# Six small DMA issues per batch moved from SyncE's queue to ScalarE's queue

## The reference

```python
x = x + xattn0(ctx, ctx, layernorm(x), ssm_kernel, D, 8)   # long convolution of k*v products, times q
x = x + ffn0(layernorm(x), gate_w, gate_b, val_w, val_b, out_w, out_b)  # activations and weights quantised, silu gate
x = x + xattn1(layernorm(x), ctx, mask, mask, Wq, bq, Wk, bk, Wv, bv)   # 16 heads of 8, softmax over 256 keys
x = x + ffn1(layernorm(x), Wc, temperature, genes, Wd, Wu, norm_w, scale)  # top 32 of 512 logits, softmax, gene mix
```

## Time and profile before

| | us |
|---|---|
| three runs | 569.9, 570.42, 573.87 (median 570.42) |
| the profiled execution | 567.63 |
| its span in the trace | 565.8 |
| busy in the span: PE, DVE, ACT, POOL | 458.6 (81%), 453.2 (80%), 350.7 (62%), 373.4 (66%) |

### The profile page before, as it was taken

The page is one execution under the profiler, slowest core; times in us unless marked ns, Lnnn a source line. Parts: engine busy times, 40 slices in busy tenths (PEclk is TensorE's granted clock), DMA queues, the critical chain, the costliest instruction groups (busy, mean ns, idle before and its releaser), DMA issues.

```text
span 565.8 us, 10986 instructions
## 1 busy us (share of the span) xinstructions
PE 458.6 (81%) x3587; PEld 257.0 (45%) x3587; DVE 453.2 (80%) x885; ACT 350.7 (62%) x607; POOL 373.4 (66%) x692
## 2 busy tenths in 40 slices
PE   1787699998987988989889898898988887778442
PEld 1576567776754543444344444444434333322110
DVE  4595579998679879799799998999989998973451
ACT  1469534333131588787788878888877877776431
POOL 6466399999887657677778777786655752341332
PEclk9987989999889899999899999999999999996875
DMA  6971011001451256565464646537636753411100
GB/s 195 370 190 25 22 56 30 17 12 48 100 115 32 64 98 137 114 113 129 91 112 110 112 124 135 103 102 158 134 96 133 150 118 102 67 28 30 51 9 19
DMA packets 93932, 54.48 MB, mean 96 GB/s; under 512 B 16610, under 2 KB 93602, under 8 KB 93876
## 3 DMA queue, kind: packets, MB, share of 16 engines
q1 hardware_dynamic: 93876, 53.78, 41.2%
HBM read 35.84 MB, written 17.42 MB: 94 GB/s over the span
## 4 chain that ended last, share of the span: by engine, by line
PE 38%; DVE 18%; issue 13%; POOL 10%; ACT 10%; DMA 6%; SPq 4%; POOLq 2%; DVEq 0%; ACTq 0%
PE pair L280 11%; DVE w_int L1669 6%; PE bank L501 5%; ACT cT L1323 5%; PE pair L488 3%; PE bank L393 3%; PE bank L530 2%; PE pair L472 2%; DMA w_raw<-w_int 2%; DVE st L1607 2%; DVE toep L1721 2%; POOL kv L949 2%; PE bank L420 2%; DMA yT<-in_x 2%; PE bank L554 1%
## 5 line engine op out<-in xcount | busy, mean ns | idle before, releaser
L1669 DVE TENSOR_REDUCE w_int<-pair 128x4 f32<-128x1024 f32 x128 | 155.2, 1213 | 23.7 <-PE pair L472 23.0
L1323 ACT ACTIVATE cT<-pair 128x1024 f32<-128x1024 f32 x128 | 131.1, 1024 | 36.1 <-PE pair L488 33.7
L280 PE MATMUL pair<-kv,toep 128*128 128x256 f32 x384 | 103.2, 414 | 8.6 <-POOL kv L949 6.3
L280 PEld LDWEIGHTS pair<-kv,toep 128*128 128x128 f32 x384 | 76.3, 208 | 25.7 <-issue 7.3
L949 POOL TENSOR_TENSOR kv<-cT 128x512 f32<-128x512 f32 x64 | 66.1, 1038 | 20.2 <-PE pair L280 14.4
L488 PE MATMUL pair<-w_raw,KS 57*128 57x256 bf16 x512 | 50.9, 277 | 33.4 <-ACT cT L1323 24.0
L501 PE MATMUL bank<-cT,v_aug 128*32 128x256 f32 x1024 | 71.1, 396 | 0.2 <-ACT qT L1331 0.2
L1494 DVE TENSOR_TENSOR prod<-pair,qT 128x512 f32<-128x512 f32 x64 | 43.9, 685 | 22.6 <-PE pair L280 21.8
L472 PE MATMUL pair<-KS,w_raw 54*128 54x256 bf16 x512 | 50.4, 275 | 10.8 <-DVE w_int L1669 10.4
L488 PEld LDWEIGHTS pair<-w_raw,KS 57*128 57x128 bf16 x512 | 16.9, 94 | 72.3 <-ACT cT L1323 54.3
L1039 POOL TENSOR_TENSOR w_raw<-w_raw 128x512 f32<-128x512 f32 x32 | 40.7, 1271 | 8.5 <-ACT w_raw L1278 7.3
(11 more groups left out here) (174 smaller groups left out, 938.7 us busy)
## 6 DMA issues: line engine op xcount, KB each, us to landing
w_raw<-scr_q SPq DMA_DIRECT2D x32, 192.0 KB
KS<-scr_k SPq DMA_DIRECT2D x32, 192.0 KB
scr_q<-w_int SPq DMA_DIRECT2D x16, 192.0 KB, 2.4
scr_k<-w_int SPq DMA_DIRECT2D x16, 192.0 KB, 2.6
scr_o<-qT SPq DMA_DIRECT2D x64, 36.0 KB
yT<-in_x SPq DMA_DIRECT2D x4, 512.0 KB, 7.6
ctx_all<-in_ctx SPq DMA_DIRECT2D x4, 512.0 KB, 8.1
x_b<-in_x SPq DMA_DIRECT2D x16, 128.0 KB, 4.5
```

Source lines behind the costliest of these rows:

```text
L280: mm = pe.matmul(bank[:, lh * n:(lh + 1) * n], toep[:, h, (lh - sh) * P:(lh - sh + 1) * P], rhs[:, sh, :], start=(sh == 0), stop=(sh == lh))
L1323: act.activation(probs[g % 4].rearrange("p j l -> p (j l)"), SC[:], ACT.Exp).then_inc(s("scores_free"), 1)
L1669: dve.tensor_reduce(neg_max[:, :, 2 * g:2 * g + 2].rearrange("p t j -> p j t"), M[:].rearrange("p (j t s) -> p j t s", t=KL, s=L), AX.X, A ...
```

## The change

`write_attention` and `load_max_rows` are moved word for word from the program of SP to that of ACT. On ACT, the four writes stand behind `copy_hidden_T(.., 1)` and ahead of `value_operand`, the two loads behind `tanh_gate(.., 0)` and ahead of `exp_left`, in both loops. The semaphores, the addresses and the sizes stay the same.

```diff
@@ sync
-                sp.wait_ge(s("o_free"), turn_o["maxima", b])
-                for j in range(2):
-                    sp.dma_start(QS[b % 3][HALF * j + ROW_MAX:HALF * j + ROW_MAX + 3, :, :],
-                                 nm_rows[3 * GRP * j:3 * GRP * (j + 1), :]).then_inc(s(f"max_rows{b % 2}_loaded"), 16)
...
-                    sp.dma_start(scr_o[k].rearrange("(q j) d l -> j d q l", j=4)[jj],
-                                 o_quad[32 * jj:32 * jj + HD + 1, :, :]).then_inc(s(f"o{k}_written"), 16)
...
-                write_attention(m - 10)
                 load_bias_terms(m - 1)
-                load_max_rows(m - 9)
@@ scalar
+            def write_attention(b):
+                if not live(b):
+                    return
+                k = b % 2
+                act.wait_ge(s("o_free"), turn_o["values", b, 3])
+                if b >= 2:
+                    act.wait_ge(s(f"o_nat{k}_loaded"), 32 * (b // 2))
+                for jj in range(4):
+                    act.dma_start(scr_o[k].rearrange("(q j) d l -> j d q l", j=4)[jj],
+                                 o_quad[32 * jj:32 * jj + HD + 1, :, :]).then_inc(s(f"o{k}_written"), 16)
+
+            def load_max_rows(b):
+                if not live(b):
+                    return
+                act.wait_ge(s("o_free"), turn_o["maxima", b])
+                for j in range(2):
+                    act.dma_start(QS[b % 3][HALF * j + ROW_MAX:HALF * j + ROW_MAX + 3, :, :],
+                                 nm_rows[3 * GRP * j:3 * GRP * (j + 1), :]).then_inc(s(f"max_rows{b % 2}_loaded"), 16)
...
                 copy_hidden_T(m - 4, 1)
+                write_attention(m - 10)
                 value_operand(m - 8)
                 copy_max_rows(m - 9)
                 tanh_gate(m - 3, 0)
+                load_max_rows(m - 9)
                 exp_left(m - 12)
```

More of the change, by code:

```diff
@@ L788, in load_stacked_qk @@
                     sp.dma_start(KS[n][rows, :, :], scr_k[k].rearrange(stacked, g=GRP, j=2)[j]).then_inc(loaded, 16)
-            def load_max_rows(b):
-                if not live(b):
-                    return
-                sp.wait_ge(s("o_free"), turn_o["maxima", b])
-                for j in range(2):
-                    sp.dma_start(QS[b % 3][HALF * j + ROW_MAX:HALF * j + ROW_MAX + 3, :, :],
-                                 nm_rows[3 * GRP * j:3 * GRP * (j + 1), :]).then_inc(s(f"max_rows{b % 2}_loaded"), 16)
[L798 to L805, removed]
-                    sp.dma_start(scr_o[k].rearrange("(q j) d l -> j d q l", j=4)[jj],
-                                 o_quad[32 * jj:32 * jj + HD + 1, :, :]).then_inc(s(f"o{k}_written"), 16)
             def load_attention(b):
```

## The result

The changed kernel took 598.8 us in the median of four runs (593.49 to 599.75), the kernel before 571.43 us in four runs beside it (569.9 to 573.87). The ratio is 1.046, 95% interval [1.042, 1.050]: 27.4 us slower. The few executions of a slower state are left out of all medians here.

A forecast was written before the change was run, and what follows sets the result against it. The prediction took a round through PE, DVE and ACT to bound the kernel, SP having time to spare. 8.4 + 3.4 + 1.0 + 4.5 = 17.3 us slower gave 587.7 us on the median, range 575 to 603.

The forecast's parts named there:

- Price of an issue: Each issue on ACT was taken to cost what SP's rows show: 0.32 us a write, 0.77 us a load.
- Held or beside: Whether ACT's issue waits for the activation ahead to end (held, 22.5 us in all) or does not (beside, 12.0 us).
- Steady rows, 1.4 us each: Rows m = 12 to 17 of the first loop: DVE's `top_first` late by 0.9 to 1.9 us a row, 8.4 us together.
- the middle that was taken: In rows m = 12 to 17, 1.4 us a row, between 0.9 for issues overlapping activations and 1.9 without overlap.
- Rows m = 10, 11 and 18: Here ACT's waits for PE cover part of the issues; together with row m = 9, 3.4 us was forecast.
- Row m = 19: The writes go in ahead of `value_operand` and delay `copy_max_rows`, which has no slack: 1.0 us taken, between 0.5 and 1.4.
- Late rows, 0.9 us each: Rows m = 20 to 24: uncovered writes on ACT delay `copy_max_rows`, the loads and PE's `scores`, 4.5 us together.
- Row m = 9, 0 to 0.5 us: Only the loads are issued by ACT in this row: 0.5 us if held, 0 if issued beside the activation.
- the 2.99 us freed become waiting: On SP, the issue time saved per row goes into its wait ahead of the load of denominators; gain nothing.
- dearer: Rival, 597 to 611 us: SP's and ACT's issues hold each other up, 1.2 us in 14 rows, or cost more; chance 0.13.
- Nothing from the clock: No time was put down for TensorE's granted clock, 1.00 in both windows; its fall would make the prediction wrong.
- almost free: Rival, 570.4 down to 564 us: issues cost ACT almost nothing and late rows' loads start earlier; chance 0.10.

The follow-up runs named there:

- e9: Changed kernel with one wait added on SP, in row m = 9 only, until batch 0's row maxima have landed; 592.43 us.
- e1: Kernel before with only the four writes (`write_attention`) moved to ACT, the loads staying on SP; 584.7 us, ratio 1.017.
- e2: Kernel before with only the two loads (`load_max_rows`) moved to ACT, the writes staying on SP; 582.8 us, ratio 1.021.
- e4: Kernel before, all its transfers left on SP, plus six spare issues of the same shapes per batch on ACT, to scratch memory; 588.08 us, ratio 1.030.
- e8: Changed kernel with eight extra matmuls of 256 columns ahead of `logits_product`, into a free bank that nobody reads; 596.63 us.
- e6: Kernel before, everything on SP, with the two loads put ahead of the four writes in both loops; 601.1 us, ratio 1.052.
- e10: Kernel before with only the first load of rows m = 20 to 24 issued by ACT, directly behind its copy; 565.62 us, ratio 0.991.
- e3: Changed kernel with SP again waiting for the copy of the row maxima, where the loads had stood, in both loops; 596.07 us.

## Why the prediction was right, and where its size was off

The forecast was 17.3 us slower, the result is 27.4. The mechanism holds: nothing is gained on SP's queue, and ACT, held by its issues, passes the delay on. The size was short by 10.1 us, for terms that the sum lacked or had near nothing.

- **Price of an issue: right.** 342 and 729 ns in the median against SP's 320 and 774. By the page "Perfetto Trace Analysis" of the Trainium skill, section "DMA Instruction — HWDGE (DVE, Sync)", the profiled time of an issue ends when the sequencer is free for its next instruction. The trace agrees for ACT's queue: the four writes end at 338.35 and `value_operand` starts at 338.46.
- **Held or beside: open in the prediction, now settled as beside.**
- **Steady rows, 1.4 us each: right in size, but not by its working.** At full clock a row takes 24.3 us in place of 23.0 (from write to write, 24.30 against 22.96), so 1.3. The way to `top_first` carries 0.96 of it, which is *beside* with its 0.9, not the middle that was taken; that the total came near 1.4 is luck. From `top_first` to `quantise_hidden` it is 12.44 us against 12.05, where nothing had been put down; DVE's L1687 alone, the product with the inverted denominators, took 0.82 us in place of 0.47 there, for a reason that no run here shows.
- **Rows m = 10, 11 and 18, some 3.4 us: about right, 2.8** (1.2, 1.0 and 0.6). The prediction's *beside* sum of 1.6 us doesn't follow from its own terms, which make 2.0. Row m = 19 was forecast at 1.0 and took 1.7 at full clock (e9).
- **Late rows, 0.9 us each: low, 1.3.** The writes' part is right: e1 pays 1.0. The step that failed is "Behind the loads, `exp_left` to `copy_logits` move 2.5 us back ... no more is added". POOL's difference of the exponentials waits for them (42.4 us in total, 14.6 before), and PE for POOL: 8 times at L539, as in e2, against twice in before and in e1. The changed kernel's chain in row m = 21:

```profile
480.58 1.28 POOL toep L1073
...
481.90 0.66 PE bank L539 x4
482.56 0.33 PE pair L488 x4
```

  PE's product L539 stands ahead of the second scores, and so the exponentials are on the round. That this wait is what the remaining 0.3 us of a late row consist of is read from the chain; no run at full clock isolates it.
- **Row m = 9, 0 to 0.5 us: wrong, 7.6.** This is the largest single error, and its root is the sentence that "the 2.99 us freed become waiting". For the issues themselves that is true. But the wait for the maxima moved with them, and in row m = 9 it had kept SP's bulk behind the small loads. e9 gives 5.1 of the 7.6 us back with one wait, 3.3 of them PE's wait, the rest with the row's clock at 1.00 again. The other 2.5 are not holding alone: e1 pays 1.5 and e4 1.1 in this row, the first load on ACT's queue is 0.6 us dear, and e9 keeps SP still until the loads have landed, longer than before. The rival *dearer* named a collision of ACT's and SP's issues, but put it in every row: it came in one.
- **Nothing from the clock: wrong.** The prediction named it as what would make it wrong, without a price. Rows 14 to 16, 19 and 22 ran at 0.84 to 0.93, besides row m = 9. Against like rows at full clock (24.3; 20.8 in e9; 19.8) they are 0.8, 1.1, 1.4, 1.2 and 1.7 us longer, 6.2 us together; row m = 12 of before had lost 1.4 in the same way. Only e8 tries the clock by itself, and neither its total nor its rows are proof. The rows of the changed kernel hold such stretches as this one in row 22 (columns as in the earlier trace rows):

```profile
503.00:509.00 6.00, 5.60 (x52) 1.82 (x56) 3.56 (x5) 3.98 (x6) 1.41 (x2) 0.50 0.42 114
```

The sum for the profiled rows: holding and what goes with it 18.9 (2.5 in row m = 9; 1.2 and 1.0; 5 x 1.3; 0.7 and 0.6; 1.7 in row m = 19; then 1.2, 1.3, 1.3, 0.9), row m = 9 crowded 5.1, clock 6.2, slow issues of writes 1.6 (0.3 in row m = 12, 1.3 in m = 13), less the 1.4 of before: 30.4, against 30.7 measured. The terms are differences of the same rows, so their sum had to come out; it shows the sizes and not the causes. That ACT's holding costs, and that SP's bulk crowds row m = 9, rest on experiments (e1, e2, e4; e9); the terms for the clock and the slow issues rest only on comparing rows. So the forecast of 17.3 was near what goes with the holding, 18.9 by rows, in part by luck in its terms; what it lacked most were row m = 9 crowded and the clock.

The rival *almost free* rested on reading the section "Issuing engines are not separate DMA queues" (the Trainium skill, page "DMA: Bandwidth & Descriptors") as leave to move issues; 33.0 us of ACT's waits for its own issues refute it for this kernel. That SP and ACT slowed each other in every row of the changed kernel is not borne out: ACT's issues have SP's median. But the mechanism that *dearer* feared exists: in e4, where both queues issue at once in each row, SP's writes rose from 320 to 452 ns in the median.

## What to carry to other kernels

Here a DMA issue held the queue of its engine for 0.3 to 0.8 us on SP and on ACT alike, and SP's writes took longer where both issued at once (e4). So it belongs on the queue that has time, and "SP waits 89 us" was the reason to leave it there. Before a wait is moved off a queue, read what stands behind it: it may be the only thing that keeps a bulk of transfers from overtaking a small one. Where two rounds have nearly the same length, making one shorter gains little, and lengthening the other costs at once (e6, e10). And a spare copy of the moved work (e4) measures its holding only as far as it doesn't meet the real work on another queue.

## What was not expected of the hardware

- Two transfers of 12 KB, issued at 192.85 among SP's bulk, let PE start 7.2 us after the end of the copy; in this row before it was 3.1, and 4.0 in e9.
- Single issues of a write take 1.1 to 1.2 us more than usual on either queue (1407 ns at most on SP, 1585 on ACT), and up to 1.6 more in other runs (1.91 us in e3), with nothing in the traces to tie them to.
- The first load that ACT's queue issues takes 1.33 us or more in each of the seven kernels that move a real load there, in whichever row it comes, and 0.73 in the median of all. On SP the first takes 0.84.
- Where SP and ACT issued writes at the same time in every row (e4), a write on SP took 452 ns in the median in place of 320; loads on ACT beside SP's own loads kept their 0.73 us.
- The granted clock fell to 0.84 to 0.93 in some rows in which PE had more waiting and not more work, and rows then grew further. Which rows differs from kernel to kernel, and before had one as well (row 12).
